# Where VectorE turns the next tile's rows in a mixture-of-experts step: behind the second block of mids, or behind the fourth

## What is computed

```python
x = x + ffn(cond(x, ...))          # x: 8 x 512 tokens of 256 channels
# cond: a filter and two quaternion rotations, linear in x
# ffn, for each of the 4096 tokens t:
h      = t @ W_in + b_in
probs  = softmax(h @ W_gate + b_gate)          # 8 experts
topv, topi = top_k(probs, 2); topv /= sum(topv)
mid    = relu(h @ W1[e] + b1[e])               # 256 -> 1024
eout   = mid @ W2[e] + b2[e]                   # 1024 -> 256
moe    = sum over the two chosen e of topv * eout
out    = moe @ W_out + b_out
```

## Time and profile before

| | us |
|---|---|
| median of 3 runs | 515.55 |
| lowest and highest | 514.03, 515.56 |
| the profiled execution, its own time | 515.1 |
| its span in the trace | 513.2 |

### The profile page before, as it was taken

How to read it: one execution, slowest core, us unless ns; L and a number is a source line. 1 busy time by engine, 2 the same in 40 slices (tenths; PEclk the granted TensorE clock), 3 DMA queues, 4 the chain that set the end, 5 groups by cost and what they waited for, 6 DMA issues and landing times.

```text
span 513.2 us, 14538 instructions
## 1 busy us (share of the span) xinstructions
PE 494.9 (96%) x4658; PEld 430.7 (84%) x4659; DVE 380.6 (74%) x742; ACT 283.2 (55%) x576; POOL 217.5 (42%) x264
## 2 busy tenths in 40 slices
PE   7889998899999999999999999999899999999997
PEld 7556687788888888888888888889799999998786
DVE  4789987677786776878768787676568887864675
ACT  3533544655666556665566665336668778780221
POOL 4500025048456384464844637435545453321121
PEclk9999999999999999999999999999999999999999
DMA  6406534846556464555645543433354445133983
GB/s 225 158 2 209 190 125 124 237 143 205 139 172 188 140 213 131 164 179 155 198 144 163 175 122 93 115 100 99 91 163 150 135 130 150 34 114 126 406 333 140
DMA packets 75812, 80.62 MB, mean 157 GB/s; under 512 B 42983, under 2 KB 61740, under 8 KB 74732
## 3 DMA queue, kind: packets, MB, share of 16 engines
q1 hardware_dynamic: 56912, 41.44, 26.2%
q0 software_dynamic: 7936, 22.29, 13.0%
q10 hardware_dynamic: 10908, 16.17, 9.9%
HBM read 53.40 MB, written 26.48 MB: 156 GB/s over the span
## 4 chain that ended last, share of the span: by engine, by line
PE 83%; DMA 5%; issue 5%; DVE 3%; ACT 2%; ACTq 1%; SPq 0%; another core or an unknown queue 0%; DVEq 0%
PE bank L1399 24%; PE bank L1386 10%; PE bank L1325 8%; PE bank L1326 7%; PE bank L1327 7%; PE bank L1218 5%; PE bank L1455 5%; PE bank L1372 4%; PE bank L1374 4%; PE bank L1373 4%; DMA gq<-rows_by_slot 2%; DMA w1s<-y_by_choice 1%; PE bank L1465 1%; PE bank L1188 1%; DMA brow<-in_L_ffn_b_in 1%
## 5 line engine op out<-in xcount | busy, mean ns | idle before, releaser
L713 ACT ACTIVATE region<-bank,b1p,cbits 128x256 f32<-128x256 f32 (+1 forms) x368 | 163.1, 522 | 131.9 <-PE bank L1327 51.7
L567 POOL DMA_INDIRECT y_by_choice<-region,dst x71 | 87.3, 1229 | 166.9 <-DVE region L1063 151.5
L1399 PE MATMUL bank<-w2s,region 128*128 x1200 | 136.0, 273 | 0.9 <-issue 0.7
L1399 PEld LDWEIGHTS bank<-w2s,region 128*128 128x128 f16 x1200 | 116.7, 98 | 16.7 <-issue 2.9
L1094 DVE TENSOR_TENSOR region<-region 128x512 f16<-128x512 f32 (+1 forms) x184 | 104.0, 575 | 27.7 <-ACT region L697 20.4
L1325 PE MATMUL bank<-region,w1s 128*128 128x256 f16 x384 | 104.7, 273 | 4.3 <-DVE region L1100 2.2
L1327 PE MATMUL bank<-region,w1s 128*128 128x256 f16 x384 | 104.7, 273 | 0.0
L1326 PE MATMUL bank<-region,w1s 128*128 128x256 f16 x384 | 104.7, 273 | 0.0
L559 POOL DMA_INDIRECT region<-z_by_token,src x71 | 71.9, 1013 | 75.4 <-DVE src L1020 50.6
L1090 DVE CAST region<-region 128x512 f16<-128x512 f32 x100 | 46.0, 460 | 52.1 <-ACT region L713 47.9
L1372 PE MATMUL bank<-region 128*128 128x128 f16 x336 | 57.5, 219 | 1.1 <-DVE region L1100 0.5
(11 more groups left out here) (267 smaller groups left out, 644.4 us busy)
## 6 DMA issues: line engine op xcount, KB each, us to landing
region<-in_L_ffn_W ACTq DMA_DIRECT2D x14, 1024.0 KB
rows_by_slot<-region SPq DMA_DIRECT2D x33, 256.0 KB
gq<-rows_by_slot SPq DMA_DIRECT2D x132, 64.0 KB
w1s<-y_by_choice SPq DMA_DIRECT2D x12, 512.0 KB, 11.1
w1s<-in_x SPq DMA_DIRECT2D x8, 512.0 KB, 8.3
z_by_token<-w1s SPq DMA_DIRECT2D x16, 256.0 KB, 2.1
region<-in_L_ffn_W SPq DMA_DIRECT2D x2, 1024.0 KB
region<-in_x SPq DMA_DIRECT2D x8, 256.0 KB
```

The lines of the kernel that those rows point to most:

```text
L567: g.indirect_dma_start(out=ybuf, out_offset=bass.IndirectOffsetOnAxis(ap=at, axis=0), in_=ysb[:, a % 2, h, :], in_offset=None).then_inc(s_ ...
L713: m = s.activation(midf[:, b, c * n:(c + 1) * n], FB[b][:, c * n:(c + 1) * n], ACT.Relu, bias=b1p[:, bass.ds(r, 1), f:f + 1].rearrange("p ...
L1399: last = mm(YB[par][:, h * D:(h + 1) * D], mids[:, par, l, b, c * TS + h * P:c * TS + (h + 1) * P], w2_at(e, w, f), start=(f == 0 and l == ...
```

## The change

Inside VectorE's step the block that turns the rows of the next tile or unit (wait for the loads, transposition, count on s_xv) is run at b == 3 where it was run at b == 1. It now stands behind all four subtractions, and in the middle tile of an expert behind the powers too; it still stands ahead of the weights' pieces, of y_out and of copy_w1.

```diff
@@ step(a) of VectorE @@
                     v.tensor_tensor(mid_at(a, 1, b), midf[:, b, 0:n], mid_at(a, 0, b),
                                     ALU.subtract).then_inc(s_mq, 1)
-                    if b == 1 and 2 <= a + 1 < NSTEP:
+                    if b == 3 and 2 <= a + 1 < NSTEP:
                         t, half = place(a + 1)
                         j8 = slice(0, 4 * H) if half is None else slice(4 * half, 4 * half + 4)
                         dve.wait_ge(s_br[t % 2], 64 * (t // 2))
```

## The result

The changed kernel took 552.2 us (median of 4 runs, 550.24 to 554.14) beside 515.55 us for the kernel before: a ratio of 1.071, with a 95% interval of 1.066 to 1.076. The profiled execution took 550.2 us, its span is 548.4 us, against 513.2: 35.2 us more. The forecast was 549.6 us in a range of 537 to 558.

A forecast was written before the change was run, and what follows sets the result against it. TensorE, busy 96% of the span, sets the time. Units 21.5 us plus tiles 12.6 us make 34.1 us on the profiled 515.1 us, 549.2 us, or 549.6 us as median; range 537 to 558 us.

The forecast's parts named there:

- Units: Unit steps: the moved transposition closes a ring of 6.41 us for 5.30, paid at 19 starts, 21.5 us in all.
- the 2 x 1.34 us: Two of the 19 unit starts, where TensorE already waited: no slack, so all of 1.34 us counts at each.
- Middle tiles: Eight middle tiles of experts: ScalarE's late last activations leave the transposition uncovered, stalling the next first layer, together 9.6 us.
- hand-over of 0.06 us: From a transposition's end to the waiting matmul's start on TensorE: 0.06 us, read from unit step 27.
- The other fifteen tiles: Remaining tile steps: later VectorE products delay ScalarE's weight load and activations, mostly hidden; 0.2 us each, 3.0 us in all.
- chain by the weight load: Tile steps: VectorE's products start 1.15 us later, ScalarE's weight load waits for them, and next-tile activations start behind it.
- The units alone pay: Rival, chance 0.15: TensorE's lateness shortens ScalarE's idle stretch, middle-tile stalls shrink to little; 539 us.
- The clock did not fall: Rival, chance 0.02: TensorE's stalls cost it the granted clock, dropping to the 1.2 GHz level; over 630 us.
- gain from earlier mids: Not-slower rival, chance 0.02: mids come earlier, as in step 1, giving back at most 4.2 us; 515 us, at best 511.

The follow-up runs named there:

- units3: Kernel before with only the unit transpositions moved behind the fourth block: 525.78 us against 505.29 us for the kernel before, ratio 1.039.
- tiles3: Kernel before with only the transpositions of steps 1 to 24 moved behind the fourth block: 506.22 us against 505.29 us, ratio 1.002.
- after_third: The changed kernel run again without further edits, in another set: 527.13 us against 507.3 us for the kernel before, ratio 1.041.
- late1: Kernel before plus four chained ScalarE copies between second and third block of the eight middle tiles: 512.01 us against 512.2 us, ratio 1.000.

## Why the prediction was right

**Units.** Right in mechanism and nearly in size: 6.38 us a step for 6.41 predicted, 19 late starts for 19, and the last subtractions did not move. The sum came to 19.6 us for 21.5. The term that was mis-sized is the 2 x 1.34 us: in steps 27 and 31 the kernel before had lost 2.2 and 0.9 us elsewhere, and the slower ring hid most of it (7.54 us became 7.86, and 6.22 became 6.38), so that the two together cost 0.5 us. Against that, step 30 grew by 1.7 us (5.30 to 7.02), which no term had. (The working also has a slip: by its own rows the moved transposition ends at 453.10 + 0.70 = 453.80, not at 453.76, which is 0.1 us of the sum.) Where these losses are absent the units cost 20.7 us, from 100.7 to 121.4.

**Middle tiles.** Right in mechanism, 11.7 us for 9.6: the eight steps grew by 1.3, 1.8, 1.6, 1.7, 1.1, 1.6, 1.9 and 0.7 us. I took the hand-over of 0.06 us from a unit; here it is 0.24 us (144.16 to 144.40; 0.14 to 0.34 in all the tile steps), and step 14, priced at nothing, lost 1.1 us. That there was anything to lose hung on ScalarE's idle stretches, which the rows showed and I took as given; that the result was measured where they are, and not where they are absent and the whole change costs 20 us, was luck.

**The other fifteen tiles.** Here a step failed in size: "by then TensorE is itself late by the middle tile's stall, which hides most of it", 0.2 us each, came to 6.5 us in all for 3.0. The chain by the weight load is as I drew it (products at 144.09, load at 146.70, activations at 147.84), but it is not what ends these steps. ScalarE's last block of step 6 was late by an idle stretch of its own (1.38 us in front of 152.06), and the transposition behind it again came last. I had taken it that ScalarE keeps up outside the middle tiles. It did not: in the kernel before its last block in these fifteen steps was done 7.4 to 9.3 us behind the first layer's start, for 8.7 to 9.4 us in the middle ones. In the changed kernel the idle time put to L1100 therefore stands in front of 20 first layers. In front of 4, 5, 7, 8, 10, 11, 13, 14, 16, 17, 19 and 20, where I had forecast little, it comes to 5.5 us. That the span grew by 35.2 us for 34.1 forecast owes something to errors that cancel, and that much is luck: the units 1.9 us under their term, the tiles 5.6 us over theirs, and 2.7 us given back at the start and the end that no term had.

**The rivals.** "The units alone pay" is what happened in two of the five sets of comparisons, the first one counted: there the whole change costs 4.1%. I had given it 0.15 as a way in which ScalarE's stretch might shrink; it isn't that they shrink, the stretches are not there from the start. The clock did not fall at stalls of 1.1 us in each unit step: it was granted at 1.00, with 104.3 us busy in 123.5. What the Trainium skill (TensorE: Matmul & The Clock Gate, "HAM oscillation — how this bites in real kernels") tells of a kernel that waits for data in every step did not set in. No gain from earlier mids showed anywhere.

## What to carry to other kernels

Price a moved instruction by a ring: from the consumer's start through everything that now stands ahead of the instruction to the consumer's next start; where that is longer than the consumer's own period, the difference is paid in every step. Find out from a step that lacks the instruction whether what stood behind it would come sooner. And ask what makes the ring long: a part that rests on another engine being late may be there in one set of runs and not in the next, as here, so that cover of a few tenths of a microsecond is none.

## What the runs showed that I had not expected

The same kernel before took 505 to 507 us in two sets and 512 to 516 us in three, at the same granted clock. In the traces the difference is idle time of ScalarE in front of the activation of a tile's block b = 1, 2 or 3 whose matmuls TensorE has finished (by the start of the block's last matmul and 0.27 us) and behind ScalarE's own activation before it. In the first profile of the kernel before there are 14 such stretches of 0.8 to 3.2 us in steps 2 to 24, 30 us in all, every one in front of block 2 or 3; in those of units3, tiles3 and after_third there is none over 0.6 us. (In front of block 0 of many tiles ScalarE stands idle in every trace, behind its own weight load or for GpSimd's table, as the program has it.)

The trace also has the times at which semaphores were counted up, and they tell what ScalarE waited for: TensorE's count of the block, s_mp, as the `<-PE bank L1327` in the timelines says. In step 5 of after_third each of the four counts is recorded 0.29 us behind the start of the block's last matmul, and ScalarE starts on blocks 2 and 3 0.13 us behind the count. In step 5 of the changed kernel's first profile the last matmul of block 2 starts at 135.90, but its count is recorded at 138.80, 2.90 us later, and that of block 3 at 138.93; ScalarE starts at 138.93, 0.13 us behind the first of them. The 14 stretches of the kernel before all end 0.13 us behind a count too. So ScalarE itself isn't slow there, and this is why the copies could run inside the stretch: in step 5 of late1 they end at 139.02 and the count comes at 139.56. Why the count comes late stays open, and so does whether the matmuls themselves ended late, as their ends are modelled; those behind them start one after the other, at most 0.23 us apart in that step of the changed kernel. Together with it stand losses in steps 27, 30 and 31 of the units.

First layer 2 started 11.0 to 12.3 us behind first layer 1 in the eight traces with step 1's transposition behind the fourth block, and 12.1 to 13.7 us in the five with it behind the second (12.1 and 12.3 us: the two ranges overlap). TensorE waits there for the row loads, which seem to land about 1 us earlier; why wasn't tried.
